# The first stage of a graph-attention kernel in another order: scores read from PSUM, the first adjacency pair loaded in two halves, low halves made on GpSimd

## The reference

```python
def _L0_gnn_ref(node_features, adjacency_matrix, W, b_W, a_vec, b_a):
    h = node_features @ W.T + b_W
    a1, a2 = (a_vec[:D_OUT], a_vec[D_OUT:])
    e = (h @ a1)[:, None] + (h @ a2)[None, :] + b_a[0]
    e = jnp.where(e > 0, e, 0.2 * e)
    scores = jnp.where(adjacency_matrix > 0, e, jnp.float32(NEG_INF))
    attention = jax.nn.softmax(scores, axis=1)
    h_prime = attention @ h
    return h_prime
h = jnp.maximum(_layernorm(x, axis=-1), 0.0)
x = x + _L0_gnn_ref(h, adj, L0_gnn_W, L0_gnn_b_W, L0_gnn_a_vec, L0_gnn_b_a)
```

## Time and profile before

| | us |
|---|---|
| three runs | 201.75, 202.73, 202.74 |
| median | 202.73 |
| the profiled execution: span, first to last instruction | 200.8 |
| the profiled execution: its own time beyond the span | not recorded; the runs lie 0.95 to 1.94 above the span |
| PE busy | 194.9 (97%) |
| DVE busy | 183.0 (91%) |
| ACT busy | 147.9 (74%) |
| GpSimd busy | 52.4 (26%) |
| DMA | 75.66 MB, 377 GB/s over the span |

### The profile page before, as it was taken

How to read it: one execution, slowest core, us unless ns; L and a number is a source line. 1 busy time by engine, 2 the same in 40 slices (tenths; PEclk the granted TensorE clock), 3 DMA queues, 4 the chain that set the end, 5 groups by cost and what they waited for, 6 DMA issues and landing times.

```text
span 200.8 us, 7230 instructions
## 1 busy us (share of the span) xinstructions
PE 194.9 (97%) x3183; PEld 189.2 (94%) x3183; DVE 183.0 (91%) x265; ACT 147.9 (74%) x192; POOL 52.4 (26%) x66
## 2 busy tenths in 40 slices
PE   7969999999999999999999999999999999999993
PEld 7648889999999999999999999999999999999993
DVE  4779999999998799897999999999999999999745
ACT  2679879898882777689988888899588888996000
POOL 1002479699995010205000000072000000510000
PEclk9999999999999999999999999999999999999999
DMA  5999999999999999999999999999999999997012
GB/s 181 376 417 418 407 403 423 421 418 415 422 432 408 418 423 419 416 421 418 415 419 423 419 418 421 421 411 421 419 418 418 415 421 416 418 383 226 6 43 66
DMA packets 15968, 75.66 MB, mean 377 GB/s; under 512 B 1600, under 2 KB 5952, under 8 KB 7616
## 3 DMA queue, kind: packets, MB, share of 16 engines
q1 hardware_dynamic: 15792, 75.06, 91.7%
q10 hardware_dynamic: 144, 0.13, 0.3%
HBM read 73.08 MB, written 2.11 MB: 374 GB/s over the span
## 4 chain that ended last, share of the span: by engine, by line
PE 91%; DMA 4%; SPq 1%; DVE 1%; issue 1%; POOL 0%
PE ps L836 29%; PE ps L834 29%; PE ps L840 29%; DMA adj_sb<-in_adj_t 4%; PE ps L808 2%; PE ps L798 2%; SPq L268 1%; SPq L273 1%; PE ps L876 1%; DVE mask L476 0%; POOL bad L788 0%; DVE rden L504 0%; DVE rg L510 0%; DVE bad L519 0%; DVE upper L576 0%
## 5 line engine op out<-in xcount | busy, mean ns | idle before, releaser
L834 PE MATMUL ps<-V,w 128*128 128x129 f16 x1024 | 174.3, 221 | 0.0
L836 PE MATMUL ps<-V,w 128*128 128x129 f16 x1024 | 174.3, 221 | 0.0
L840 PE MATMUL ps<-V,w 128*128 128x129 f16 x1024 | 174.3, 221 | 0.0
L379 ACT ACTIVATE mask<-adj_sb 128x1024 bf16<-128x1024 int32 x126 | 125.5, 1056 | 28.6 <-DMA adj_sb<-in_adj_t 28.6
L459 DVE SCALAR_TENSOR_TENSOR w<-g_row,pairs,mask 128x1024 f32<-128x1024 f32 x96 | 120.5, 1320 | 5.5 <-ACT mask L379 3.6
L834 PEld LDWEIGHTS ps<-V,w 128*128 128x128 f16 x1024 | 100.2, 98 | 1.5 <-ACT H L340 0.7
L836 PEld LDWEIGHTS ps<-V,w 128*128 128x128 f16 x1024 | 100.2, 98 | 1.0 <-issue 1.0
L840 PEld LDWEIGHTS ps<-V,w 128*128 128x128 f16 x1024 | 100.2, 98 | 0.0
L459 DVE SCALAR_TENSOR_TENSOR w<-ps,pairs,mask 128x1024 f32<-128x1024 f32 x31 | 37.4, 1267 | 0.0
L785 POOL TENSOR_TENSOR xT<-xT,x_sb 128x512 f32<-128x512 f32 x6 | 11.5, 1932 | 79.8 <-ACT xT L394 79.8
L739 POOL TENSOR_TENSOR x_sb<-x_sb,b_row 128x512 f32<-128x512 f32 x8 | 10.0, 1301 | 0.0
(11 more groups left out here) (93 smaller groups left out, 63.8 us busy)
## 6 DMA issues: line engine op xcount, KB each, us to landing
adj_sb<-in_adj_t SPq DMA_DIRECT2D x64, 1024.0 KB, 10.3
xT<-in_x_t SPq DMA_DIRECT2D x8, 256.0 KB, 7.5
x_sb<-in_x_p SPq DMA_DIRECT2D x3, 512.0 KB, 10.9
g_row<-g_dram SPq DMA_DIRECT2D x1, 1536.0 KB, 10.3
out<-xT SPq DMA_DIRECT2D x3, 512.0 KB, 9.9
x_sb<-in_x_p SPq DMA_DIRECT2D x2, 256.0 KB, 4.2
out<-xT SPq DMA_DIRECT2D x1, 192.0 KB, 3.4
out<-xT SPq DMA_DIRECT2D x3, 64.0 KB, 1.6
```

Source lines behind the costliest of these rows:

```text
L379: nc.scalar.activation(mask[:, m % MASKS, r], adj_sb[:, m % HELD, r], ACT.Relu, scale=CONNECTED).then_inc(mask_ready, 1)
L834: nc.tensor.matmul(sums[:, bank, a, :], w16[:, m % SLOTS, col:col + P, 1], V[:, jt, 0, 0:NF], start=(jt == 0 and a == 0), stop=False, skip ...
L836: nc.tensor.matmul(sums[:, bank, a, :], w16[:, m % SLOTS, col:col + P, 1], V[:, jt, 1, 0:NF], start=False, stop=False, skip_group_check=True)
L840: last = nc.tensor.matmul(sums[:, bank, a, :], w16[:, m % SLOTS, col:col + P, 0], V[:, jt, 0, 0:NF], start=False, stop=(jt == NT - 1), ski ...
```

## The change

- **DMA order.** x 0 comes ahead of xT 1. The first adjacency pair is loaded as two transfers of half the size, the first right behind x 1 (semaphore adj_begun), the second behind xT 2, xT 3 and x 2; adj 1 comes ahead of xT 4.
- **Scores of tiles 0 to 7** are read by DVE from PSUM in two instructions (`first_scores`) ahead of ACT's copies of the chunks, which now wait for them. ACT loads its table of exponentials ahead of the copies, and takes the two roots in the other order.
- **PE.** The product for cc moves behind h 1. Centre 2 and 3 both come behind the transpose of the maxima. The eight transposes come ahead of h 2. The first pair comes behind h 2 and **ahead of h 3 and centre 4**; it is written as `first_pair`, which multiplies the high parts of the first side first, then the low parts, then the second side. All later pairs keep their places relative to their neighbours by one chunk: h 4 and centre 5 now stand behind whole(1), h 5 and centre 6 behind whole(2), h 6 and centre 7 behind whole(3), and h 7 behind whole(4).
- **DVE.** `products` and `lows` are gone from it. All eight statistics of set 2 stand in one place, behind `weigh_first(1)` and ahead of `weigh(0, 1)`.
- **GpSimd** makes the low parts of chunk 0 (`first_lows`) and both parts of chunk 1 (`halves(1)`), ahead of `deviations(2, 3)`.
- **ACT** drops `highs(1)`; weights(0) stands between take 0 and take 1.

```diff
                 load_xt(0)
+                load_x(0)
                 load_xt(1)
-                load_x(0)
                 load_x(1)
+                sp.dma_start(adj_sb[:, 0, 0:GC], adj_t[0, :, 0:GC]).then_inc(adj_begun, 16)
                 load_xt(2)
+                load_xt(3)
                 load_x(2)
-                load_xt(3)
-                load_adj(0)
+                sp.dma_start(adj_sb[:, 0, GC:2 * GC], adj_t[0, :, GC:2 * GC]).then_inc(adj_loaded[0], 16)
+                load_adj(1)
                 load_xt(4)
-                load_adj(1)
...
                 def take_chunk(c):
                     act.wait_ge(h_done, c + 1)
+                    if c < 2:
+                        act.wait_ge(scores_ready, 1)
...
                 roots_part()
+                nc.scalar.activation(warm[:], zero_col[:], ACT.Exp)
                 take_chunk(0)
+                weights(0)
                 take_chunk(1)
-                nc.scalar.activation(warm[:], zero_col[:], ACT.Exp)
                 relu_chunk(2)
-                weights(0)
-                relu_chunk(3)
                 highs(0)
                 first_mask()
+                relu_chunk(3)
                 take_chunk(2)
                 mask_part(1)
                 take_chunk(3)
                 relu_chunk(4)
-                highs(1)
                 mask_part(2)
...
+                def first_scores():
+                    dve.wait_ge(h_done, 2)
+                    dve.wait_ge(std_ready, 2)
+                    for c in range(2):
+                        r = slice(c * CT, (c + 1) * CT)
+                        of = ps[:, H_BANK[c]:H_BANK[c] + 2, 0:2 * (2 + DOUT)].rearrange("p k (a n) -> p k a n", a=2)
+                        by = rstd[:, 1, r].rearrange("p (k a n) -> p k a n", k=2, n=1).to_broadcast([P, 2, 2, 2])
+                        ins = nc.vector.tensor_tensor(st[:, r, :].rearrange("p (k a) n -> p k a n", k=2),
+                                                      of[:, :, :, 0:2], by, ALU.mult)
+                    ins.then_inc(scores_ready, 1)
...
+                step_(nc.vector.tensor_scalar(rstd[:, 2, 0:GI], rstd[:, 1, 0:GI], gg[:, 1:2], None, ALU.mult))
+                inverse_scales(0)
                 early_mask()
                 pack(0)
                 scale_weights(0)
-                products(0)
                 dve.wait_ge(pairs_ready, 1)
                 weigh_first(0)
-                lows(0)
                 weigh_first(1)
+                statistics(2)
                 weigh(0, 1)
-                statistics(2, 5, 8)
                 weigh(1, 0)
                 weigh(1, 1)
-                products(1)
-                lows(1)
                 scores(1)
...
+                def first_lows():
+                    pool.wait_ge(scaled_ready, 1)
+                    pool.wait_ge(ones_ready, 1)
+                    pool.wait_ge(h_ready, 1)
+                    step(nc.gpsimd.tensor_tensor(prod[:, 0, :, :], H[:, 0:CT, H0:HC],
+                                                 evr[:, 0:CT].rearrange("p (n a) -> p n a", a=1).to_broadcast([P, CT, NF]),
+                                                 ALU.mult))
+                    pool.wait_ge(high_ready, 1)
+                    nc.gpsimd.tensor_tensor(V[:, 0:CT, 1, 0:NF], prod[:, 0, :, :], V[:, 0:CT, 0, 0:NF],
+                                            ALU.subtract).then_inc(low_ready, 1)
+
+                first_lows()
+                halves(1)
                 deviations(2, 3)
...
                 centre_chunk(1)
+                pe.wait_ge(wa_ready, 1)
                 h_chunk(0)
-                pe.wait_ge(norm_ready, 1)
                 h_chunk(1)
-                centre_chunk(2)
+                nc.tensor.matmul(ps[:, 6, 0:2], wp[:, BW:BW + 1].to_broadcast([P, P]), wp[:, AV:AV + 2], start=True,
+                                 stop=True).then_inc(cc_done, 1)
                 pe.wait_ge(t_limits, 1)
                 nc.tensor.transpose(ps[:, G_BANK + 1, 0:P], tt[:, 0:1].to_broadcast([P, P]), ident[:]).then_inc(t_spread, 1)
+                centre_chunk(2)
                 centre_chunk(3)
-                h_chunk(2)
...
                     last.then_inc(rows_spread, 1)
+                h_chunk(2)
+                first_pair()
                 h_chunk(3)
                 centre_chunk(4)
-                pe.wait_ge(h_ready, 3)
-                whole(0)
+                whole(1)
                 h_chunk(4)
                 centre_chunk(5)
-                whole(1)
+                whole(2)
                 h_chunk(5)
                 centre_chunk(6)
-                whole(2)
+                whole(3)
                 h_chunk(6)
                 centre_chunk(7)
-                whole(3)
+                whole(4)
                 h_chunk(7)
-                for m in range(4, NM - ENDS):
+                for m in range(5, NM - ENDS):
```

More of the change, by code:

```diff
@@ L746, in halves @@
                     r = slice(c * CT + k0, c * CT + k1)
-                    part = 1 if c < 4 else 2
+                    part = (0, 0, 1, 1, 2, 2, 2, 2)[c]
                     pool.wait_ge(scaled_ready, part + 1)
@@ L842, in products, with first_pair @@
                     return last
+                def first_pair():
+                    pe.wait_ge(high_ready, 1)
+                    pe.wait_ge(w_begun, 1)
+                    for k in range(GI):
+                        if k == CT:
+                            pe.wait_ge(w_ready, 1)
+                        bank, a = sums_at(0, k)
+                        nc.tensor.matmul(sums[:, bank, a, :], w16[:, 0, k * P:(k + 1) * P, 1], V[:, 0, 0, 0:NF],
+                                         start=(a == 0), stop=False, skip_group_check=True)
+                        nc.tensor.matmul(sums[:, bank, a, :], w16[:, 0, k * P:(k + 1) * P, 0], V[:, 0, 0, 0:NF],
+                                         start=False, stop=False, skip_group_check=True)
+                    pe.wait_ge(low_ready, 1)
+                    for k in range(GI):
+                        bank, a = sums_at(0, k)
+                        nc.tensor.matmul(sums[:, bank, a, :], w16[:, 0, k * P:(k + 1) * P, 1], V[:, 0, 1, 0:NF],
+                                         start=False, stop=False, skip_group_check=True)
+                    pe.wait_ge(w_ready, 2)
+                    for k in range(GI):
+                        bank, a = sums_at(0, k)
+                        high = w16[:, 0, GC + k * P:GC + (k + 1) * P, 1]
+                        low = w16[:, 0, GC + k * P:GC + (k + 1) * P, 0]
+                        nc.tensor.matmul(sums[:, bank, a, :], high, V[:, 1, 0, 0:NF], start=False, stop=False,
+                                         skip_group_check=True)
+                        nc.tensor.matmul(sums[:, bank, a, :], high, V[:, 1, 1, 0:NF], start=False, stop=False,
+                                         skip_group_check=True)
+                        last = nc.tensor.matmul(sums[:, bank, a, :], low, V[:, 1, 0, 0:NF], start=False, stop=False,
+                                                skip_group_check=True)
+                    last.then_inc(mm_done, 1)
                 def whole(m):
```

75 lines of the change are left out of this document (25 added, 50 removed).

## The result

The changed kernel takes 205.96 us (median of 4, 205.25 to 206.16), the kernel before beside it on the same chip 202.24 us (median of 4, 201.69 to 202.74): a ratio of 1.0176, 95% interval 1.0144 to 1.0209. By this ratio it is slower by 3.6 us. The profiled execution has a span of 204.6 us and a time of 206.11 us, against a span of 200.8 us before. Two executions in a slow state are in no figure here, one of the kernel before (336.92 us) and one of the kernel that has the loads of the change alone (711.87 us).

A forecast was written before the change was run, and what follows sets the result against it. PE was taken as the bound, full from the first pair to the tail, so only its gaps count: 1.0 + 0.3 + 1.9 = 3.2 us on 202.73 gives 205.9 us, range 203.7 to 207.3.

The forecast's parts named there:

- three gaps: PE waits for DVE's weights: pair 0 +1.0 us, pair 3 +0.3, pairs 6 and 7 +1.9; chance 0.70.
- part 1: Start up to the first mask on DVE: mask starts at 11.09 us instead of 12.74, bounds 10.6 to 11.6.
- part 2: Pair 0: PE waits some 1.8 us for the second side's weights; +1.0 us, bounds +0.5 to +1.5.
- the mark: Moment when PE has done pair 0, h 3 and c 4: 19.75 us before, forecast 20.78.
- part 3: Pair 3: its weights' chain from c 5 takes 5.70 us against PE's 5.39; +0.3 us, bounds 0 to 0.6.
- part 4: Pairs 6 and 7: chain from take 7 takes 7.36 us against PE's cover of 5.44; +1.9, bounds 1.3 to 2.3.
- the two other outcomes: Whole kernel: time within about 0.5% (1.0 us) of no change, chance 0.11; faster by more, 0.06.
- (a): Whole kernel not slower: DVE keeps ahead of PE, pair 0 runs through, 0.75 us less, 202.0; chance 0.08.
- (b): Only the first gap, in pair 0; the chain to pair 7 is covered: +1.0 to +1.3, 203.9; chance 0.08.
- (c): Only the gap at pairs 6 and 7; the statistics cost nothing: +1.9, 204.6; chance 0.07.
- (d): First half of adj lands late, DVE waits for it again, mask at up to 12.7: 207.5; chance 0.03.
- (e): PE's clock falls to 1.2 GHz at the new 1.8 us gap in pair 0: 209.1; chance 0.04.

The follow-up runs named there:

- both faults undone: Changed kernel with the statistics behind weigh(0, 1), PE's order as before, and h 3 and centre 4 between the first pair's sides: ratio 1.0042 to the kernel before.
- the first experiment: Changed kernel with DVE's eight statistics of tiles 8 to 15 moved behind weigh(0, 1): ratio 1.0111 to the kernel before.
- Experiments two and three: Changed kernel with, in two, ACT's mask 6 ahead of take 7 (ratio 1.0095 to the kernel before); in three, PE's order as before (1.0074).

## Why the prediction was right

Its forecast, slower by three gaps at 205.9 us, came about: each gap stands where it was put, behind the instructions that were named. One step, part 1, was mis-sized, and that the median was met so closely is in part luck. By its steps:

| step | forecast | measured |
|---|---|---|
| scores from PSUM start | 9.18 | 10.02 |
| mask starts | 11.09 | 11.90 |
| mask to second side's weights | 6.35 | 6.27 |
| PE's wait ahead of them | 1.8 | 1.65 |
| part 2, the mark | +1.0 | +1.66 |
| part 3, pair 3 | +0.3 | +0.31 |
| part 4, pairs 6 and 7 | +1.9 | +1.82 |
| span | 204.0 | 204.6 |
| median | 205.9 | 205.96 |

**Part 1** was mis-sized: the mask came 0.8 us later than worked out, beyond the upper bound of 11.6. From the scores to the mask it took 1.88, forecast 1.91; what was late is the start of the scores, by 0.84. In the profiled execution PE came last. In the kernel before its first centring was

```profile
5.24 1.11 PE L798 MATMUL ps<-xT,centre 128*128 128x512 f32 x2
```

With the 0.2 us for the cc product it should have started at 5.04. It started at 5.39 and took 1.66 us, which is 0.90 later at its end. So the pace of PE at the start, which I had taken from one execution, was not a constant.

But a quick centring would not have saved the step. With the statistics later, and with PE's order as before, both with the loads of the change, the first centring took 1.16 and 1.10 us, and the scores still started at 10.13 and 9.89. There DVE waits for x of tiles 4 to 7: the scores need 1/std, and that needs these statistics. From the timeline of DVE of the second of the two:

```profile
7.92 0.87 DVE L550 BATCH_NORM_STATS2 stats<-x_sb 128x6 f32<-128x128 f32 x4 [1.08 <-DMA x_sb<-in_x_p]
...
9.89 0.24 DVE L568 TENSOR_TENSOR st<-ps,rstd 128x8 f32<-128x8 f32 x2
```

With both faults undone in the changed kernel that wait is 0.54 us and the scores start at 9.34; with the loads of before there is no such wait, and they start at 9.03, 0.15 ahead of the forecast. So the step let the scores wait for PE alone and put the arrival of x of tiles 4 to 7 at nothing; of the loads it weighed only those of adj and of x of tiles 8 to 15. In the profiled execution of the change no wait for this x shows, since PE was later; what held its other executions no trace tells.

**Part 2** carried this error on, and with it went beyond its own bound: +1.66 against at most +1.5, and pair 1 starts at 21.41 where 20.8 was its sign. Less the 0.8 of the mask it is 0.86, close to the +1.0. Its other sign, PE idle for 1.5 to 2 us behind eight statistics in a row, is there. The signal from DVE to PE, put at 0.12 us, took 0.06 (18.17 to 18.23). That the place of the statistics is what is wrong is shown by the first experiment.

**Part 3** came out to a hundredth, **part 4** to a tenth. The chain from pair 5's beginning to pair 7's is 46.23 - 38.97 = 7.26, forecast 7.36, against the cover of 5.44 us. Experiments two and three confirm the two ingredients of part 4, ACT's order and PE's: changing either takes the waits away or most of them. For part 3 PE's order is tested by the third; no run takes the eight statistics out of its chain.

**Why the median was met better than the span.** The forecast kept the 1.93 us that lay between the profiled span and the median of the runs shown. The profiled execution of the changed kernel lies 1.5 us above its span, and is 0.15 above the median. The two small errors, 0.6 us each, cancel, and that is luck: the median of three runs to which the forecast added its 3.2 us was 202.73, with a fourth run it is 202.24, and the medians lie 3.72 apart. By its own list the chances of a slower kernel add up to 0.88 where the prediction has 0.86, and those of the two other outcomes to 0.08 and 0.04 where it has 0.11 and 0.06.

**The rivals.** (a) wanted the second side's weights by 15.8; they were there at 18.17, so it fell. (b) and (c) each left one of the gaps out; both gaps are there. (d) fell, as the early mask has no wait for DMA. (e) fell: behind the wait of 1.65 us the matmuls start 0.06 us apart (18.23, 18.30) and the granted clock shows full. The Trainium skill, page "TensorE: Matmul & The Clock Gate", section "HAM oscillation — how this bites in real kernels", tells of a kernel whose bursts each start slow behind waits that are longer than this one; this trace shows that the wait of 1.65 us did not slow the burst behind it.

**What the prediction did not see**: that even without the two faults hardly anything was to be gained. It treated the wait of 1.03 us for the first block as one that a better order could remove. Two of the kernels with contiguous halves in the place of the whole block removed it and one cut it to 0.34 us, and none is faster by more than its measurement tells. For one of them the trace shows where the gain goes, the wait for the next blocks behind which relu 6 stands. In the profiles of the other two PE waits for nothing there, and why they are no faster stays open.

## What to carry to other kernels

When a step is moved on one engine, follow the whole queues of the engines that wait for it, not only the step: here one copy (take 7) that came a pair later on PE held a mask, a weighing, a packing and a pair, three engines on. A wait for a load at the start of a full queue was here, in one profile, only the first of several; before removing such a wait, look at what the same engine waits for in the next pairs. And when a load is brought forward, list who needs those that it passes.

## What the runs showed of the hardware

**Half rows are slower to load than whole blocks.** In all kernels whose first pair was loaded as 4 KB halves of rows of 8 KB, the DMA rate dips for 2 us and more while the first half comes in (174 to 305 GB/s, from 6 to 8 or from 9 to 11 us, in eight profiles): 279 and 283 GB/s above, and in the changed kernel

```profile
6.00:7.00 1.00, 1.00 (x3) 0.37 (x2) 0.62 (x6) 0.00 (x0) 0.00 (x0) 1.00 0.98 293
7.00:8.00 1.00, 1.00 (x6) 0.51 (x5) 0.68 (x4) 0.60 (x1) 0.00 (x0) 1.00 0.86 246
```

The dip moved with the halves when they were put later (242 and 305 GB/s from 9 to 11 us), and was gone in the three where the same bytes lay contiguous (403 to 422 GB/s from 9 to 11 us). The kernel before, with a whole block, moves 336 and 361 GB/s from 6 to 8 us and 408 to 455 from 8 to 11. Shown is that the layout makes the dip; how is not.

**PE's first centring has no fixed length.** With the same warming matmuls ahead of it on PE it took 1.10 to 1.16 us in eight profiles, 1.66 in that of the change, and 2.05 or 2.06 in three others, of which two are kernels made from the one before whose list for PE is the same as there. The granted clock is recorded as full in all of them, though the length is up to double that of the later centrings (1.02 us). Double would fit the lower of the two clock levels, 1.2 GHz, by the reading of pace that the prediction makes in its rival (e), but the recorded clock does not confirm it. In the execution of the kernel with relu 6 ahead the mark is at 21.03, 1.3 us behind the earlier trace rows, with two slow centrings; that is more than half of what the spans of one kernel differ by (200.2 to 202.6 us for the kernel before); that the two belong together is a guess.
